# FP4 rounding in the FFN with ScalarE's square as the rounding number, and the variance by one aggregate instruction

## What is computed

```python
def fp4_quant_dequant(x):            # _GRID 0 .5 1 1.5 2 3 4 6, _MID the midpoints between
    xb = x.reshape(shape[:-1] + (shape[-1] // BLOCK, BLOCK))          # BLOCK = 16
    scale = jnp.maximum(jnp.max(jnp.abs(xb), axis=-1, keepdims=True) / 6.0, 1e-12)
    xn = xb / scale
    q = _GRID[jnp.searchsorted(_MID, jnp.abs(xn))] * jnp.sign(xn) * scale
    return q.reshape(shape)
...
x = x + cross_attention(layernorm(x), ctx_1024)
x = x + self_attention(layernorm(x))          # 16 heads of 16, causal
x = x + ffn(layernorm(x))    # gate, up: fp4_linear 256 -> 704; h = silu(gate) * up; down: fp4_linear 704 -> 256
```

## Time and profile before

| what | value |
|---|---|
| time, median of 3 runs (lowest, highest) | 627.73 us (627.31, 629.44) |
| profiled execution, first to last instruction | 627.5 us |
| PE busy | 554.8 us, 88% of the span |
| DVE busy | 531.7 us, 85% |
| ACT busy | 207.2 us, 33% |
| POOL busy | 45.0 us, 7% |
| mean granted TensorE clock, share of full | 0.964 |

### The profile page before, as it was taken

How to read it: one execution, slowest core, us unless ns; L and a number is a source line. 1 busy time by engine, 2 the same in 40 slices (tenths; PEclk the granted TensorE clock), 3 DMA queues, 4 the chain that set the end, 5 groups by cost and what they waited for, 6 DMA issues and landing times.

```text
span 627.5 us, 16121 instructions
## 1 busy us (share of the span) xinstructions
PE 554.8 (88%) x6390; PEld 434.1 (69%) x6390; DVE 531.7 (85%) x1067; ACT 207.2 (33%) x429; POOL 45.0 (7%) x84
## 2 busy tenths in 40 slices
PE   4999999999999999997448888888899888888885
PEld 4888888888888888885335656666676666666553
DVE  5868999999999999998256889999999998999984
ACT  1323323322333323321025444443444433443120
POOL 4001000000000000000011110011111101101100
PEclk9999999999999999999758979999999998999898
DMA  8990111211101111121000000000000000000000
GB/s 253 328 303 3 67 67 67 67 67 67 67 17 51 67 67 67 67 67 69 4 0 3 1 3 9 8 8 8 0 8 8 8 8 8 8 8 8 10 9 17
DMA packets 13798, 30.97 MB, mean 49 GB/s; under 512 B 976, under 2 KB 10704, under 8 KB 11728
## 3 DMA queue, kind: packets, MB, share of 16 engines
q1 hardware_dynamic: 13776, 30.67, 15.1%
HBM read 28.57 MB, written 2.10 MB: 49 GB/s over the span
## 4 chain that ended last, share of the span: by engine, by line
issue 30%; DVE 10%; PE 6%; ACT 2%; POOL 2%; DVEq 0%; POOLq 0%; ACTq 0%
PE bank L1123 2%; DVE f_xn L1348 2%; PE bank L1101 1%; POOL f_rstd L1014 1%; DVE f_xn L1449 1%; DVE f_amax_x L1446 1%; PE bank L1145 1%; ACT a_kblocks L1245 1%; DVE f_pow_x L1462 1%; DVE f_pow_x L1457 1%; DVE f_h L1366 1%; DVE f_inv_x L1448 1%; DVE f_amax L1374 1%; PE bank L1071 0%; PE bank L1168 0%
## 5 line engine op out<-in xcount | busy, mean ns | idle before, releaser
L316 PEld LDWEIGHTS bank<-x_xcT,xwk 128*128 128x128 f32 x512 | 61.0, 196 | 2.8 <-issue 1.1
L316 PE MATMUL bank<-x_xcT,xwk 128*128 128x128 f32 x512 | 61.4, 279 | 1.4 <-ACT x_xcT L408 1.4
L357 PE MATMUL bank<-xwo,x_oT 128*128 128x256 f32 x256 | 59.5, 387 | 1.1 <-ACT x_oT L425 1.1
L338 PE MATMUL bank<-xwv,x_xcT 128*128 128x512 f32 x128 | 59.2, 605 | 1.2
L307 PE MATMUL bank<-x_xcT,xwq 128*128 128x128 f32 x512 | 59.8, 275 | 0.0
L307 PEld LDWEIGHTS bank<-x_xcT,xwq 128*128 128x128 f32 x512 | 58.5, 192 | 0.0
L357 PEld LDWEIGHTS bank<-xwo,x_oT 128*128 128x128 f32 x256 | 48.6, 195 | 7.9 <-issue 1.6
L1101 PE MATMUL bank<-wdT,f_hqT 128*128 128x256 f32 x192 | 47.4, 398 | 3.0 <-ACT f_hqT L1221 3.0
L1245 ACT ACTIVATE a_kblocks<-bank,head_rows 128x256 f32<-128x256 f32 x128 | 48.6, 499 | 0.0
L534 DVE STREAM_TRANSPOSE x_probsT<-x_probs 32x512 f32<-32x512 f32 x64 | 44.8, 701 | 1.7
L437 ACT COPY x_k_blocks<-bank 64x512 f32<-64x512 f32 x32 | 18.6, 581 | 79.9 <-PE bank L316 79.7
(11 more groups left out here) (152 smaller groups left out, 966.5 us busy)
## 6 DMA issues: line engine op xcount, KB each, us to landing
x_ctx_slab<-in_ctx_dram SPq DMA_DIRECT2D x16, 1028.0 KB, 4.8
out_dram<-f_out SPq DMA_DIRECT2D x16, 128.0 KB, 1.7
xall<-in_x_dram SPq DMA_DIRECT2D x1, 1280.0 KB, 17.3
x_first_keys<-in_ctx_dram SPq DMA_DIRECT2D x4, 320.0 KB, 12.5
xwk<-in_L_xattn_w_k_dram SPq DMA_DIRECT2D x1, 1024.0 KB, 5.0
xwq<-in_L_xattn_w_q_dram SPq DMA_DIRECT2D x1, 1024.0 KB, 7.1
xwv<-in_L_xattn_w_v_dram SPq DMA_DIRECT2D x1, 1024.0 KB, 10.3
xwo<-in_L_xattn_w_o_dram SPq DMA_DIRECT2D x1, 1024.0 KB, 12.8
```

The costliest lines, as they stand in the source:

```text
L316: last = nc.tensor.matmul(bank[2 + j // 4][:, (j % 4) * P:(j % 4 + 1) * P], xwk[:, k, j * P:(j + 1) * P], xcT[:, KD + k, :], start=(k == 0 ...
L338: last = nc.tensor.matmul(bank45[:, half, :], xcT[:, KD + k, :], xwv[:, k, half * 512:(half + 1) * 512], start=(k == 0), stop=(k == KD - 1))
L357: last = nc.tensor.matmul(bank67[:, 0, 0:D], oT[:, j, :], xwo[:, j, :], start=(j == 0), stop=(j == XP - 1))
```

## The change

For the FFN's two quantizations the exponent mask and the magic number made from it are dropped. ScalarE squares the scaled number instead, times a constant (`grid`, f_grid_x and f_grid), and VectorE makes 1.5 * 2^22 plus this square minus the number, and then once more with the result (`to_grid`, `from_grid`), in one instruction of the same kind each. The factor just below one moves from `add_magic` to the scaling (`in_units`). So VectorE has two instructions fewer for each of the two tiles, and between the scaling and `to_grid` it waits for ScalarE. `add_out` now stands ahead of `to_grid` on VectorE; before, it stood between `add_magic` and `subtract_magic`. The four instructions of `variance` become one `bn_aggr`. The rounding of the weights is as before.

```diff
 ScalarE
+                    def grid(scaled, out, ready, done, t):
+
+                        act.wait_ge(ready, t + 1)
+                        nc.scalar.activation(out, scaled, ACT.Square, scale=GRID_SLOPE).then_inc(done, 1)
+
...
                         if gate and attend:
                             tanh(t - 2)
+                        if norm:
+                            grid(f_xn[:], f_grid_x[:], s_f_xs, s_f_xg, t - 1)
                         if project:
                             copy_qk(t + 1)
+                        if gate:
+                            grid(f_hn[:], f_grid[:], s_f_hs, s_f_hg, t - 2)
...
 VectorE
                             x_step(nc.vector.bn_stats(f_stats[:], tile_of(t - 1)))
-                            variance(nc, x_step, f_stats, f_mv)
-                            nc.vector.tensor_scalar(f_ve[:], f_mv[:, 3:4], LN_EPS, None, ALU.add).then_inc(s_f_ve, 1)
+                            dve.sem_inc(s_f_st, 1)
+                            x_step(nc.vector.bn_aggr(f_mv[:], f_stats[:]))
+                            nc.vector.tensor_scalar(f_ve[:], f_mv[:, 1:2], LN_EPS, None, ALU.add).then_inc(s_f_ve, 1)
...
-                            scale_blocks(nc, x_step, xv, xv, f_amax_x[:], f_scale_x[:], f_inv_x[:], NB)
+                            block_scales(nc, x_step, xv, f_amax_x[:], f_scale_x[:], f_inv_x[:])
+                            in_units(nc, xv, f_inv_x[:], NB, xv, s_f_xs)
...
                         if norm:
-                            take_exponents(nc, x_step, f_xn[:], f_pow_x[:])
-                            take_magic(nc, x_step, f_pow_x[:])
-                            add_magic(nc, x_step, f_xn[:], f_pow_x[:])
+                            dve.wait_ge(s_f_xg, t)
+                            to_grid(nc, x_step, f_xn[:], f_grid_x[:])
...
                         if norm:
-                            subtract_magic(nc, x_step, f_xn[:], f_pow_x[:])
+                            from_grid(nc, x_step, f_xn[:], f_grid_x[:])
...
-                            f_step.later(nc.vector.tensor_tensor(blocks(f_hn[:]), blocks(f_h[:]),
-                                                                 f_inv[:].unsqueeze(2).to_broadcast([P, FB, QBLK]),
-                                                                 ALU.mult))
-                        if gate:
-                            take_exponents(nc, f_step, f_hn[:], f_pow[:])
+                            in_units(nc, blocks(f_h[:]), f_inv[:], FB, blocks(f_hn[:]), s_f_hs)
...
-                        if gate:
-                            take_magic(nc, f_step, f_pow[:])
-                            add_magic(nc, f_step, f_hn[:], f_pow[:])
                         if down and (attend or not gate):
                             add_out(t - 3)
                         if gate:
-                            subtract_magic(nc, f_step, f_hn[:], f_pow[:])
+                            dve.wait_ge(s_f_hg, t - 1)
+                            to_grid(nc, f_step, f_hn[:], f_grid[:])
+                            from_grid(nc, f_step, f_hn[:], f_grid[:])
...
+def in_units(nc, w, inv, nb, out, done):
+    nc.vector.scalar_tensor_tensor(out=out, in0=w, scalar=BELOW_ONE,
+                                   in1=inv.unsqueeze(2).to_broadcast([P, nb, QBLK]),
+                                   op0=ALU.mult, op1=ALU.mult).then_inc(done, 1)
+
+
+def to_grid(nc, step, xn, square):
+    step.later(nc.vector.scalar_tensor_tensor(out=xn, in0=square, scalar=GRID_BASE, in1=xn,
+                                              op0=ALU.add, op1=ALU.subtract))
+
+
+def from_grid(nc, step, xn, square):
+    step.sync()
+    step.later(nc.vector.scalar_tensor_tensor(out=xn, in0=square, scalar=GRID_BASE, in1=xn,
+                                              op0=ALU.add, op1=ALU.subtract))
```

More of the change, by code:

```diff
@@ L20 @@
 BELOW_ONE = 1.0 - 2.0 ** -24
+GRID_BASE = 1.5 * 2.0 ** 22
+GRID_SLOPE = (0.14 * 2.0 ** 22) ** 0.5
 QBLK = 16
@@ L922, in perceiver_layer @@
             a_res = psb("a_res", [P, D])
-            f_stats, f_mv, f_ve, f_rstd = psb("f_stats", [P, 6]), psb("f_mv", [P, 4]), psb("f_ve", [P, 1]), \
+            f_stats, f_mv, f_ve, f_rstd = psb("f_stats", [P, 6]), psb("f_mv", [P, 2]), psb("f_ve", [P, 1]), \
                 psb("f_rstd", [P, 1])
             f_xn = psb("f_xn", [P, D])
-            f_pow_x = psb("f_pow_x", [P, D])
+            f_grid_x = psb("f_grid_x", [P, D])
             f_amax_x, f_scale_x, f_inv_x = psb("f_amax_x", [P, NB]), psb("f_scale_x", [P, NB]), psb("f_inv_x", [P, NB])
-            f_pow = psb("f_pow", [P, F])
+            f_grid = psb("f_grid", [P, F])
             f_amax, f_scale, f_inv = psb("f_amax", [P, FB]), psb("f_scale", [P, FB]), psb("f_inv", [P, FB])
@@ L953, in perceiver_layer @@
             s_f_xr = sem("f_x_rounded")
+            s_f_st = sem("f_stats_ready")
+            s_f_xs, s_f_xg = sem("f_x_scaled"), sem("f_x_grid_ready")
+            s_f_hs, s_f_hg = sem("f_h_scaled"), sem("f_h_grid_ready")
             s_f_xq, s_f_xt, s_f_xc = sem("f_xq_ready"), sem("f_xq_turned"), sem("f_xqT_ready")
@@ L958, in perceiver_layer @@
             N_PARTS = ((0, 1), (1, T))
-            A_STEPS, X_STEPS, F_STEPS = 3, 1 + 3 + 1 + 8, 2 + 8
+            A_STEPS, X_STEPS, F_STEPS = 3, 1 + 2 + 1 + 3 + 2, 2 + 3 + 2
             def steps(eng, step):
@@ L1430, in _, with block_scales @@
                     steps(dve, step)
[L1433 to L1444, removed]
+def block_scales(nc, step, w, amax, scale, inv):
     step(nc.vector.tensor_reduce(amax, w, AX_X, ALU.max, apply_absolute_value=True))
@@ L1448, in scale_blocks @@
     step(nc.vector.reciprocal(inv, scale))
+def scale_blocks(nc, step, w, xn, amax, scale, inv, nb):
+    block_scales(nc, step, w, amax, scale, inv)
     step(nc.vector.tensor_tensor(xn, w, inv.unsqueeze(2).to_broadcast([P, nb, QBLK]), ALU.mult))
```

## The result

The changed kernel takes 611.73 us (median of 4 runs, 609.85 to 614.19) beside 627.65 us for the kernel before (627.31 to 629.44, 4 runs). The ratio is 0.9726, 95% interval [0.9697, 0.9756]: 2.7% faster. The profiled execution took 609.85 us with a span of 608.4 us, so 1.45 us lie around the span; all four runs show 1.4 to 1.5. It is the shortest of the four.

What follows compares the result with a forecast made beforehand. VectorE was taken to bound the kernel, 16.7 of 17.2 us a turn. Savings of 16.9 in the loop, 0.9 ahead and 3.4 behind, 21.2 off a 627.5 span, gave 606.3, plus 0.2: 606.5 us, range 601 to 613.5.

Steps and rivals of the forecast that it cites:

- ScalarE is late: Rival in the loop, chance 0.18: hidden square up to 1.4 us or a_kblocks slip; turn 16.2 to 16.5, 610 to 613.5.
- VectorE sets the pace before: Loop of the kernel before: VectorE sets the pace with 16.7 of 17.2 us a turn; TensorE has some 1.7 to spare.
- a ring through down, f_out and two roundings: Changed loop: f_hq, turn on TensorE, products, down, f_out, two roundings, next f_hq; a turn of 15.91 us, before 17.20.
- The 1.0 us that I gave back for a slow turn: Loop: of 17.9 us saved in 12 turns, 1.0 deducted for a slow-clock turn that may come again, leaving 16.9.
- The square fits behind a_kblocks: Loop, ScalarE: hidden square takes 0.8 us after the eight a_kblocks, from 13.0 to 13.8 after f_hq, 0.2 to spare.
- The variance saves 0.50: VectorE, each turn: four variance instructions, 0.74 us, become one aggregate, some 0.24 with its wait; saving 0.50.
- Ahead of the loop, 0.9: Steps 1 and 2: step 2 wins 1.8 us, the x square delaying copy_qk in step 1 loses 0.9; net 0.9.
- Behind the loop, 3.4: Steps behind the loop: step 15 saves 2.1 us, step 16 saves 1.6, step 17 loses 0.6; together 3.4 saved.
- What lies around the span is 0.2 us: Whole kernel: the median lies 0.2 us above the profiled span, so 606.3 becomes 606.5.
- TensorE alone at 15.5: Rival in the loop, chance 0.10: a turn falls to TensorE's busy 15.5 us; total 601.7.
- second table load: Rival on ScalarE, chance 0.03: Square needs another table, two loads a turn; 618 us or unchanged.
- the clock fell more: Rival, chance 0.06: TensorE's clock falls more often, three to six more falls; 611 to 616 us.

Runs made afterwards that it cites:

- e1: The kernel before with only the variance's four instructions replaced by one aggregate instruction: 621.33 us, ratio 0.9891.
- e2: The changed kernel with the four instructions of the variance put back: 617.96 us, ratio 0.9837 to the kernel before.
- e3: The changed kernel with add_out (f_out) moved between to_grid and from_grid: 607.99 us, ratio 0.9658 to the kernel before.
- e5: The changed kernel with ScalarE's square of the hidden tile done twice, first into an unread buffer: 616.87 us, ratio 0.9794 to the kernel before.
- e8: The changed kernel with the hidden square behind six of the eight a_kblocks, ahead of the last two: 610.50 us, ratio 0.9702 to the kernel before.
- e7: The changed kernel with the x square of step 16 and a hidden square reordered among ScalarE's copies behind the loop: 607.55 us, ratio 0.9662 to the kernel before.
- e9: The changed kernel with add_out between the roundings and the hidden square behind six of eight a_kblocks: 602.24 us, ratio 0.9581 to the kernel before.

## Why the prediction was right, and where it was off

The forecast was 606.5 us in a range of 601 to 613.5; the median is 611.73. Its point was 5.2 us too low, and the measured time is outside the 604 to 609 that the forecast gave itself. That the whole range holds it is partly luck: its upper part, 610 to 613.5, was there for the rival "ScalarE is late", a turn of 16.2 to 16.5, which did not happen. The turn was 16.09 for another reason, and the rest came from the tail.

- *VectorE sets the pace before; the variance counts in full there.* Right (e1).
- *Afterwards a ring through down, f_out and two roundings holds the turn, at 15.91.* Right in mechanism: e2 takes 0.64 us of VectorE's slack without moving the turn, e3 breaks the ring and moves it by 0.31, e5 and e8 show the square to be off the path in this order. The term that was mis-sized in the loop is the handover from the end of down to `f_out`, 0.26 us and not 0.1 (490.68 to 490.94); the three instructions took 2.19 against 2.17. That is 16.09 for 15.91, 2.2 us in twelve turns. The 1.0 us that I gave back for a slow turn did not come in this execution: 16.9 forecast, 15.54 measured.
- *The square fits behind a_kblocks.* Right, at 0.85 us and with 0.57 to spare.
- *The variance saves 0.50.* It is 0.41; the increment that stands alone takes the rest. In the changed kernel's loop that makes no difference.
- *Ahead of the loop, 0.9.* 1.42. The x square did hold up `copy_qk` in step 1, at a price of 0.4 and not 0.9; step 2 gained 1.73 of the 1.8.
- *Behind the loop, 3.4.* **This step failed**: the tail got 0.6 us longer. Step 15 gained its 2.1 (17.07 to 14.88 between two `f_hq`), but I had costed steps 16 and 17 by VectorE's chain alone and not asked what stands behind the waiting square in ScalarE's queue: copies that TensorE waits for. Between `f_hq` of 15 and 16 only 0.42 us were gained where I had 1.6, the next stretch was 2.33 longer (9.06 to 11.39), and the last 0.87, with the turn of the last `f_hq` at a granted clock of 0.50 (1.54 us) where it had 1.00 before (0.88 us). e7 shows the queue's order to be worth 3.4 us; the last stretch stays 0.9 longer than before in e7 too (11.26 us). With e7's order the tail is 2.9 us shorter than in the kernel before, where 3.4 were forecast.
- *What lies around the span is 0.2 us.* It is 1.4 to 1.5 in every run; I had set a profiled span against a median of other executions. That is 1.2 us.
- The balance of the 5.2 us: tail 4.0, loop 1.4 and what lies around the span 1.2 too little; less 0.5 ahead of the loop and 2.7 by which the unchanged first stretch came out shorter in the profiled run; and then 1.9 more by which that run lies under its median. That makes 5.3, the rest is rounding. The 2.7 that nothing in the change explains hides part of the miss.

Of the rivals, "TensorE alone at 15.5" did not happen and rested on a floor that e9 undercuts; "ScalarE is late" was 0.57 us away; no second table load appears; the clock fell more in the tail (0.93 and 0.67 in the last two stretches, 1.00 and 0.82 before), which is the part of that rival that came true.

## What to carry to other kernels

When work moves to an engine with time to spare, read the queue there at every place where the order differs, the written-out steps too: a new instruction that waits is a gate for all that stand behind it, and in the tail here it cost about what the change should have won. When an engine is relieved, look for the ring that closes next before counting its saving: the saving was 2.0 us a turn, the ring let 1.1 through, and moving two instructions within their queues gave 0.9 more. And a neighbour's busy time in a trace with waits is not its floor.

## What the runs showed of the hardware that was not expected

- TensorE's busy time for the same products of a turn is 15.44 us in the kernel before, 15.14 in the changed kernel and 15.15 in e9. Before, it waits twice inside the turn, 0.23 us ahead of turning `a_o` and 1.44 ahead of the scores. Ahead of such a wait a product counts as busy to its modelled end; without one the next starts sooner: in the changed kernel the turn of `a_o` starts at 491.38, 0.16 us before the row ahead of it ends.
- One semaphore increment that stands alone between two dependent VectorE instructions lengthens their distance from 0.46 to 0.57 us, in all 16 steps (before against the changed kernel, e1 and e2).
- ScalarE's square of 128x704 takes 0.79 us in the trace when ScalarE was idle before it and 0.85 when it follows a busy ScalarE at once, where it starts before the one ahead ends; done twice in a row, start to start is 0.68.
- In step 1 the normalisation `f_xn` took 0.76 us before and 0.37 after. GpSimd's addition (0.73 us) started 0.11 us ahead of it before (346.35 and 346.46) and ran beside all but its last part; after, it started 0.53 us ahead (343.14 and 343.67), and only its last 0.2 us lay beside. The twelve traces hold 192 such normalisations, and all fit: 0.72 to 0.81 us in the 170 that have 0.57 us or more of the addition beside them, 0.37 in the 10 with 0.2, and 0.41 to 0.42 in step 16, which has no addition (597.73 us before, 575.44 after). So in every turn of the loop this instruction is some 0.3 us longer than alone. No run moved the addition on purpose.
